# Node tables by one matmul and one-hots by one activation, laid out by DMA

## The chip, the cores and the metric

The kernel runs on one core of a Trainium2 chip. The metric is the device time of one execution in microseconds (us), and lower is better. The engines are TensorE (PE), VectorE (DVE), ScalarE (ACT), GpSimd (POOL) and SyncE (SP), which only issues DMAs and waits.

## The reference

The input x is 16 images of 96 channels, 64 x 64 points, float32. Two layers follow each other.

```python
# layer 0: graph convolution in windows of 8 x 8 points
y = affine(conv1x1(x, fc1_w, fc1_b), fc1_s, fc1_t)
nodes = window_partition(y)                    # 64 windows an image, each 64 nodes x 96
idx = knn_idx(nodes, 9)                        # nearest 9, by normalised dot products
x_j = nodes[idx]; x_i = nodes[:, None]
feat = concat([x_i, x_j - x_i])                # 192
h = gelu((feat @ ew.T + eb) * es + et)         # 192 outputs
h = max over the 9 neighbours
x1 = affine(conv1x1(h, fc2_w, fc2_b), fc2_s, fc2_t) + x
# layer 1: inverted bottleneck
h = relu(bn(conv1x1(x1, w1)))                  # 576 channels
h = relu(bn(depthwise_3x3(h, wd)))
out = x1 + bn(conv1x1(h, w2))
```

## The kernel before

The unit of work is a pair of windows, P, 128 nodes. There are 32 pairs an image and 512 in all. A loop over images holds one iteration of every engine per pair, in an order written out by hand, and only semaphores join the engines. Layer 1 works in strips of 16 rows (four an image), so a strip lasts eight pairs. Its jobs are put at fixed distances after the strip's first pair by tables such as `W1_AT`, `RELU2_AT`, `W2_AT`, `UPPER_AT`, `STORE_AT`. The place of a pair is its number mod 8. A place decides which of these jobs come in its iteration.

The edge convolution is split: every node has a row V (for itself as a neighbour) and a row U (as the centre), each 192 numbers. Neighbour k of node n gives V[idx] + U[n], and that sum is a matmul with a one-hot matrix: `VU` holds, per window, V on 64 partitions and U on the other 64. `MV` (128 partitions x 512 columns per window) holds the one-hots of the neighbours on 64 partitions and an eye matrix, written once in the set-up, on the other 64. In window 0 the one-hots stand on partitions 0 to 63, in window 1 on 64 to 127, and `VU` is arranged to match. Both are double-buffered by pair.

For one pair these steps follow each other over several iterations:

- `scores` (L588, three pairs ahead), then VectorE's eight largest, their indices and a feature; `feature_transpose` two pairs ahead.
- `expand` (L614), one pair ahead: eight small matmuls put, per neighbour, a number into the PSUM bank `pvu` (seen as `pone`) that is zero or below except where the index hits.
- `onehot` (L800) on ScalarE: two activations of 64 partitions, from that bank into the two halves of `MV`.
- `values` (L624), one pair ahead: four products, each of 64 nodes with V's or U's weights (192 columns), placed on the half of the same bank `pvu` where `VU` wants them. It waits for `onehot`, since that frees the bank.
- `vu_copy` (L812) on ScalarE: one activation of 128 x 384 from the bank into `VU`. The next `expand` waits for it.
- `gather` (L639), in three parts: parts 0 and 1 give 128 outputs of window 0 and window 1, part 2 the other 64 of both. ScalarE's GELU follows each part and VectorE takes the maxima.

An iteration on TensorE is: scores(P+3), gather part 0 of P, feature_transpose(P+2), the first of the shared jobs, expand(P+1), gather part 1, the other shared jobs, values(P+1), gather part 2. The shared jobs (`misc_jobs`: fc1, sums of squares, norms, the self terms, fc2, w1, w2) take three PSUM banks in turn.

GpSimd issues the accumulating DMAs: `acc<-tapped` (L429, 512 KB, four a strip), `res<-x` (L438) and `x<-in_x_dram` (L407), two of each a strip. SyncE issues everything else: the input loads, the norms' trip through DRAM and back, two copies a strip between halves of the 576 - 512 = 64 leftover channels (L374 to L381, `hpad` group 4) and the output stores (L389). ScalarE waits for the half-group copies by `kept_half` and for the stores by `store_done`.

## Time and profile before

| | |
|---|---|
| median of 3 runs | 4107.27 us (4103.47 to 4110.96) |
| profiled execution | 4102.94 us |
| its span, first to last instruction | 4101.1 us |
| mean granted TensorE clock | 0.987 |
| busy: TensorE, VectorE, ScalarE, GpSimd | 95%, 93%, 90%, 23% |
| DMA, mean | 66 GB/s |

A row of a group gives the line of the kernel, the engine, the tiles (out<-in), the shapes, the number of instructions, their busy time and mean duration, and the idle time of the engine just before them with what ended it. PE is the matmul itself and PEld its weight load. Each float32 product is two matmul instructions in the trace. The chain is the work that ended last, followed backwards. SPq is the DMA queue of SyncE. Durations of matmuls are modelled ends, so the distance between starts says more than a sum of them.

### The profile page before, as it was taken

To read this page: it belongs to the slowest core of one execution; us is meant where nothing else is said; L and a number is where in the kernel's file an instruction comes from. 1 tells how busy PE (TensorE), PEld (TensorE's weight loads), DVE (VectorE), ACT (ScalarE), POOL (GpSimd) and SP (SyncE) were. 2 spreads that over 40 slices of the span, in tenths; PEclk is the share of its full clock that TensorE was granted. 3 is DMA by queue.
4 is the path that set the end of the run, shared out by engine and by line. 5 is a ranking of instruction groups with operands and counts; after the bars stand their busy time and mean duration, and the time that the engine had idled before them with its cause. 6 is when DMAs were issued, how large, how long until landed. Compare 5 with 4: busy or idle time off the path is not lost.

```text
span 4101.1 us, 79112 instructions
## 1 busy us (share of the span) xinstructions
PE 3901.0 (95%) x22752; PEld 2049.0 (50%) x22752; DVE 3821.5 (93%) x5162; ACT 3694.2 (90%) x6805; POOL 931.2 (23%) x1060
## 2 busy tenths in 40 slices
PE   4999999999999999999999999999999999999984
PEld 2445555455554555555555455555555455555542
DVE  2599999999999999999999999999999999999996
ACT  3899999999998999989999899989999899999983
POOL 0122222122222122222122222122222122222113
PEclk9999999999999999999999999999999999999996
DMA  1133342333333333343333333333333333433333
GB/s 50 24 64 76 58 88 51 67 76 66 73 73 66 60 75 73 58 80 57 69 75 66 73 61 75 62 69 76 62 79 57 70 66 67 81 61 59 62 66 65
DMA packets 100114, 272.31 MB, mean 66 GB/s; under 512 B 14946, under 2 KB 23394, under 8 KB 93476
## 3 DMA queue, kind: packets, MB, share of 16 engines
q0 software_dynamic: 65536, 184.58, 26.4%
q1 hardware_dynamic: 34116, 82.27, 7.5%
q8 instruction: 204, 3.34, 0.3%
q14 instruction: 258, 2.11, 0.2%
HBM read 77.68 MB, written 25.69 MB: 25 GB/s over the span
## 4 chain that ended last, share of the span: by engine, by line
PE 68%; DVE 11%; issue 9%; ACT 9%; DMA 1%; SPq 0%; POOL 0%; DVEq 0%; ACTq 0%; POOLq 0%
PE pg L648 18%; PE pmisc L576 9%; PE pg L651 8%; PE pvu L635 8%; DVE acc L1032 7%; PE pmisc L562 7%; PE pmisc L519 3%; PE pmisc L512 2%; PE pvu L621 2%; ACT MV L807 2%; PE pmisc L578 2%; DVE hid L1010 2%; PE pmisc L542 2%; PE pmisc L547 2%; ACT tapped L844 1%
## 5 line engine op out<-in xcount | busy, mean ns | idle before, releaser
L1032 DVE SCALAR_TENSOR_TENSOR acc<-hpad,w,acc 128x1024 f32<-128x1024 f32 (+1 forms) x2304 | 2618.2, 1160 | 33.5 <-issue 16.3
L648 PE MATMUL pg<-MV,VU 128*128 128x512 f32 x2048 | 1149.2, 643 | 40.7 <-ACT VU L815 29.8
L824 ACT ACTIVATE g<-pg 128x512 f32<-128x512 f32 x1536 | 912.5, 594 | 127.9 <-PE pg L651 81.4
L1010 DVE TENSOR_REDUCE hid<-g 128x192 f32<-128x1536 f32 x512 | 892.6, 1743 | 0.0
L429 POOL DMA_DIRECT2D acc<-tapped x256 | 241.3, 943 | 2106.8 <-DVE acc L1032 1818.8
L807 ACT ACTIVATE MV<-pvu,cst 64x512 f32<-64x512 f32 x1024 | 696.0, 680 | 11.8 <-PE pvu L621 5.0
L576 PE MATMUL pmisc<-acc,w 128*96 128x256 f32 x2048 | 497.1, 386 | 49.0 <-ACT acc L854 34.1
L651 PE MATMUL pg<-MV,VU 128*64 128x512 f32 x2048 | 527.5, 592 | 0.0
L562 PE MATMUL pmisc<-x,w 96*128 96x512 f32 (+1 forms) x1024 | 518.3, 608 | 7.0 <-ACT hpad L766 7.0
L635 PE MATMUL pvu<-wVU,y 97*64 97x192 f32 x4096 | 446.7, 339 | 21.8 <-ACT MV L807 21.2
L576 PEld LDWEIGHTS pmisc<-acc,w 128*96 128x96 f32 x2048 | 331.5, 165 | 262.6 <-issue 154.9
L766 ACT ACTIVATE hpad<-pmisc,sh,sc 128x512 f32<-128x512 f32 (+1 forms) x560 | 421.6, 770 | 16.7 <-PE pmisc L562 9.0
L635 PEld LDWEIGHTS pvu<-wVU,y 97*64 97x64 f32 x4096 | 248.7, 136 | 300.8 <-issue 164.0
L854 ACT ACTIVATE acc<-acc,shd,scd 128x1024 f32<-128x1024 f32 (+1 forms) x320 | 360.6, 1147 | 29.6 <-DMA acc<-tapped 29.6
L648 PEld LDWEIGHTS pg<-MV,VU 128*128 128x128 f32 x2048 | 309.5, 191 | 87.3 <-issue 59.5
L837 ACT ACTIVATE acc<-hpad,w 128x1024 f32<-128x1024 f32 (+1 forms) x320 | 338.9, 1060 | 0.2
L600 PEld LDWEIGHTS pscore<-xn,xs 97*64 97x64 f32 x2048 | 145.9, 137 | 325.2 <-issue 315.6
L562 PEld LDWEIGHTS pmisc<-x,w 96*128 96x128 f32 x1024 | 185.7, 193 | 239.5 <-issue 214.2
L815 ACT ACTIVATE VU<-pvu 128x384 f32<-128x384 f32 x512 | 250.2, 489 | 51.2 <-PE pvu L635 40.5
L844 ACT ACTIVATE tapped<-hpad,w 128x1024 f32<-128x1024 f32 x256 | 292.2, 1141 | 0.0
L621 PEld LDWEIGHTS pvu<-featT,c 128*128 128x128 f16 x4096 | 183.0, 100 | 217.8 <-issue 214.7
L976 DVE MAX8 top<-pscore 128x8 f32<-128x64 f32 x512 | 115.9, 226 | 163.1 <-PE pscore L602 161.7
(101 smaller groups left out, 4447.6 us busy)
## 6 DMA issues: line engine op xcount, KB each, us to landing
acc<-tapped POOLq DMA_DIRECT2D x256, 512.0 KB, 4.9
xin<-in_x_dram SPq DMA_DIRECT2D x32, 768.0 KB, 5.8
invb<-rows_dram SPq DMA_DIRECT2D x32, 768.0 KB
x<-in_x_dram POOLq DMA_DIRECT2D x128, 192.0 KB, 4.4
res<-x POOLq DMA_DIRECT2D x128, 192.0 KB, 5.0
out_dram<-res SPq DMA_DIRECT2D x128, 192.0 KB, 3.2
hpad<-hpad SPq DMA_DIRECT2D x112, 33.0 KB, 1.8
g<-in_consts_dram SPq DMA_DIRECT2D x1, 640.0 KB
```

The costliest lines, as they stand in the source:

```text
L562: last = nc.tensor.matmul(ps[:, 0:(hi - lo) * W], w1T[:, gr * 128:(gr + 1) * 128], x1[:, lo:hi, :], start=True, stop=True)
L576: nc.tensor.matmul(ps[0:C, 0:4 * W], w2T[:, gr, :], acc[:, par, sums_of(gr, q * 4 * W, 4 * W)], start=(gr == 0), stop=False)
L635: last = nc.tensor.matmul(pvu[h:h + 64, O * w:O * (w + 1)], nodes, wVU[:, k, :], start=True, stop=True)
L648: last = nc.tensor.matmul(ps[:, :], VU[:, r, part, 0:ONE128], cols[part], start=True, stop=True)
L651: last = nc.tensor.matmul(ps[64 * w:64 * w + 64, :], VU[:, r, w, ONE128:O], cols[w], start=True, stop=True)
L766: nc.scalar.activation(hpad[:, gr, r0:r1, 1:W + 1], ps[:, 0:(r1 - r0) * W].rearrange("p (row col) -> p row col", col=W), ACT.Relu, bias=sh ...
L807: last = nc.scalar.activation(MV[h:h + 64, p % 2, w, :].rearrange("p (n k) -> p n k", k=KN), pone[h:h + 64, :, :].rearrange("p k n -> p n ...
L824: nc.scalar.activation(g[:, p % 2, part, :, :], pg[(3 * p + part) % 2][:, :].rearrange("p (n k) -> p n k", k=KN), ACT.Gelu).then_inc(gelu_ ...
L837: nc.scalar.activation(acc[:, t % 2, sums_of(gr, 0, rows * W)].rearrange("p (row col) -> p row col", col=W), hpad[:, gr, 0:rows, 0:W], ACT ...
L854: nc.scalar.activation(acc[:, par, sums_of(gr, 0, n)], acc[:, par, sums_of(gr, 0, n)], ACT.Relu, bias=shd[:, gr:gr + 1], scale=scd[:, gr:g ...
L1010: nc.vector.tensor_reduce(hid[:, c % 2, j, :, :], g[:, r], op=ALU.max, axis=AX.X).then_inc(hid_ready, 1)
L1032: nc.vector.scalar_tensor_tensor(out=dst, in0=src, scalar=wk, in1=dst, op0=ALU.mult, op1=ALU.add).then_inc(tap_done, 1)
```

## The change

- `values` is one product of 128 nodes with the weights of V and U side by side (384 columns). The result has the nodes on the partitions: window 0 on 0 to 63, window 1 on 64 to 127.
- `onehot` is one activation of 128 partitions, into a new tile `onehots`.
- `vu_copy` writes a new tile `nodesVU` instead of `VU`.
- SyncE puts both in place: `move_tables` with four DMAs (64 partitions x 192 numbers, 48 KB each) into `VU`, and `move_onehots` with two DMAs (64 partitions x 512 numbers, 128 KB each) into `MV`. The one-hots now stand on partitions 0 to 63 for both windows and the eye on 64 to 127. `onehots` and `nodesVU` are single, so `onehot` and `vu_copy` wait for the last moves.
- `values` and `vu_copy` run two pairs ahead instead of one. The bank `pvu` is still used in the order expand, values.
- The first gather of a pair waits for the two moves' semaphores instead of ScalarE's.
- In SyncE's order the moves come first in an iteration; the output stores and the upper half-group copy are one pair later, and the norms' trip is split over two pairs.
- `hpad` is stored as one run of rows, with 10 instead of 18 for the half group. The indexing follows (`rows_of`). VectorE's `last` gets a lower bound of 3.

```diff
@@ -42,7 +42,7 @@
 W1_AT = {-1: [(0, 0), (0, 1), (0, 2)], 0: [(1, 0)], 1: [(1, 1), (1, 2)], 2: [(2, 0), (2, 1), (2, 2)],
          3: [(3, 0), (3, 1), (3, 2)], 4: [(4, 0), (4, 2)]}
 KEEP_AT = {-2: (0, 1), 2: (2, 3)}
-UPPER_AT, LOWER_AT = {2: FULL}, {5: FULL}
+UPPER_AT, LOWER_AT = {3: FULL}, {5: FULL}
 TAP0_AT = {}
 TAP0_LATE = {0: [0], 1: [1], 3: [2], 4: [3], 5: [4]}
 RELU2_AT = {6: [0], 7: [1], 10: [2, 4], 11: [3]}
@@ -53,7 +53,7 @@
 SELF_AT = {2: 'self_half', 3: 'self_full', 4: 'self_half', 5: 'self_full'}
 ORDER = ('ssq', 'fc1', 'inv', 'self_full', 'self_half', 'fc2', 'w1', 'w2')
 ADD_AT = {o + 1: q for o, q in W2_AT.items() if q % 2 == 1}
-STORE_AT = {o + 2: q for o, q in W2_AT.items() if q % 2 == 1}
+STORE_AT = {o + 3: q for o, q in W2_AT.items() if q % 2 == 1}
 FIRST = [(g, k) for k in range(1, TAPS - 1) for g in (0, 1)]
 SECOND = [(2, 1), (3, 1), (2, 2), (3, 2), (4, 1), (2, 3), (3, 3), (4, 2), (2, 4), (4, 3), (3, 4), (2, 5), (4, 4), (3, 5),
           (2, 6), (4, 5), (3, 6), (2, 7), (4, 6), (3, 7), (4, 7), (4, 8)]
@@ -188,6 +188,11 @@
     return slice(g * STRIP * W + start, g * STRIP * W + start + n)
 
 
+def rows_of(g, first, end):
+
+    return slice((STRIP + 2) * g + first, (STRIP + 2) * g + end)
+
+
 def due(count):
 
...
@@ -263,6 +268,8 @@
         featT = sb("featT", [128, 2, NODES], f16)
         VU = sb("VU", [128, 2, 2, O])
         MV = sb("MV", [128, 2, 2, KN * NODES])
+        onehots = sb("onehots", [128, KN * NODES])
+        nodesVU = sb("nodesVU", [128, 2, O])
         g = sb("g", [128, 2, 3, NODES, KN])
         gself = sb("gself", [128, 2, PPC, 3, NODES])
         gflat = g[:, 0].rearrange("p c n k -> p (c n k)")
@@ -270,7 +277,7 @@
         r97 = g[0:C + 1, 1].rearrange("p c n k -> p (c n k)")[:, 0:3 * O]
         hid = sb("hid", [128, 2, PPC, 3, NODES])
         x1 = sb("x1", [C, H, W])
-        hpad = sb("hpad", [128, 5, STRIP + 2, PADW])
+        hpad = sb("hpad", [128, FULL * (STRIP + 2) + STRIP // 2 + 2, PADW])
         acc = sb("acc", [128, 2, (2 * FULL + 1) * STRIP * W // 2])
         tapped = sb("tapped", [128, FULL, STRIP * W])
         res = sb("res", [C, 2, CW])
@@ -298,6 +305,7 @@
             "score_ready", "top8_ready", "idx_ready", "a_ready", "feat_ready"))
         featT_ready, featT_evac, onehot_in, onehot_ready = (sem(n) for n in (
             "featT_ready", "featT_evac", "onehot_in", "onehot_ready"))
+        onehot_moved, vu_moved = sem("onehot_moved"), sem("vu_moved")
         vu_ready, vu_evac, gather_ready, gelu_done, chunk_ready = (sem(n) for n in (
             "vu_ready", "vu_evac", "gather_ready", "gelu_done", "chunk_ready"))
         kept, kept_half = sem("kept"), sem("kept_half")
@@ -337,13 +345,16 @@
             sp.dma_start(c16f[:, :], consts16).then_inc(param_load, 16)
             load_half(0, 1)
 
-            def broadcast_norms(b, p, bi, h):
-
-                n = 2 * bi + h
+            def store_norms(b, p, bi, h):
+
                 fb, fp = when(b, p, ROWS_AT - 8)
                 sp.wait_ge(misc_evac, job_at(fb, fp, "inv", 4 * h))
                 sp.sem_inc(sp_passed, 1)
                 sp.dma_start(rows_dram.rearrange("k (r n) -> (k r) n", n=128), norm_rows[:, :]).then_inc(rows_stored, 16)
+
+            def broadcast_norms(bi, h):
+
+                n = 2 * bi + h
                 sp.wait_ge(rows_stored, 16 * (n + 1))
                 sp.sem_inc(sp_passed, 1)
                 if due(count := 4 * n):
@@ -353,11 +364,37 @@
                 sp.dma_start(rows[0:C, :], rows_dram[0:1, :].to_broadcast([C, 4 * CW])).then_inc(rows_loaded, 16)
                 sp.dma_start(rows[C:C + 1, :], rows_dram[1:2, :]).then_inc(rows_loaded, 16)
 
+            def move_tables(P, p):
+
+                if due(count := 3 * P - 3):
+                    sp.wait_ge(gather_ready, count)
+                sp.sem_inc(sp_passed, 1)
+                if due(count := P + 1):
+                    sp.wait_ge(vu_evac, count)
+                sp.sem_inc(sp_passed, 1)
+                for k in range(2):
+                    for w in range(2):
+                        sp.dma_start(VU[64 * k:64 * k + 64, p % 2, w, :], nodesVU[64 * w:64 * w + 64, k, :]).then_inc(vu_moved, 16)
+
+            def move_onehots(P, p):
+
+                if due(count := P + 1):
+                    sp.wait_ge(onehot_ready, count)
+                sp.sem_inc(sp_passed, 1)
+                for w in range(2):
+                    sp.dma_start(MV[0:64, p % 2, w, :], onehots[64 * w:64 * w + 64, :]).then_inc(onehot_moved, 16)
+
             def image(b, p0, p1):
                 for p in range(p0, p1):
+                    P = PAIRS * b + p
                     h = 1 if p < 16 else 0
                     if p % 16 == ROWS_AT and valid(b if h else b + 1, B):
-                        broadcast_norms(b, p, b if h else b + 1, h)
+                        store_norms(b, p, b if h else b + 1, h)
+                    if p % 16 == ROWS_AT + 1 and valid(b if h else b + 1, B):
+                        broadcast_norms(b if h else b + 1, h)
+                    if valid(P + 1, NPAIRS):
+                        move_tables(P + 1, p + 1)
+                        move_onehots(P + 1, p + 1)
 
                     if p in (1, 8) and valid(b, B) and valid(b + 1, B):
                         h = p // 8
@@ -371,14 +408,14 @@
                             sp.wait_ge(tap_done, count)
                         sp.sem_inc(sp_passed, 1)
                         if t == 0:
-                            sp.dma_start(hpad[0:64, gr, 0, 1:W + 1], zrow[0:64, :]).then_inc(kept_half, 16)
+                            sp.dma_start(hpad[0:64, (STRIP + 2) * gr + 0, 1:W + 1], zrow[0:64, :]).then_inc(kept_half, 16)
                         else:
-                            sp.dma_start(hpad[0:64, gr, 0:2, :], hpad[64:128, gr, 8:10, :]).then_inc(kept_half, 16)
+                            sp.dma_start(hpad[0:64, rows_of(gr, 0, 2), :], hpad[64:128, rows_of(gr, 8, 10), :]).then_inc(kept_half, 16)
                     for o, t, s, gr in due_in(LOWER_AT, b, p):
                         fb, fp = when(b, p, o - w1_slot(gr, 0))
                         sp.wait_ge(misc_evac, job_at(fb, fp, "w1", (gr, 0)))
                         sp.sem_inc(sp_passed, 1)
-                        sp.dma_start(hpad[64:128, gr, 0:2, :], hpad[0:64, gr, 8:10, :]).then_inc(kept_half, 16)
+                        sp.dma_start(hpad[64:128, rows_of(gr, 0, 2), :], hpad[0:64, rows_of(gr, 8, 10), :]).then_inc(kept_half, 16)
 
                     for o, t, s, q in due_in(STORE_AT, b, p):
                         sp.wait_ge(out_sum[q // 2], 16 * (s + 1))
...
@@ -615,7 +652,7 @@
                 if due(count := P + 1):
                     pe.wait_ge(featT_evac, count)
 
-                if due(count := P):
+                if due(count := P + 1):
                     pe.wait_ge(vu_evac, count)
                 for k in range(KN):
                     last = nc.tensor.matmul(pone[:, k, :], LK[:, k, :], featT[:, p % 2, :], start=True, stop=True)
@@ -625,15 +662,10 @@
 
                 c, o = pair(p)
 
-                if due(count := P + 1):
+                if due(count := P):
                     pe.wait_ge(onehot_ready, count)
-                for w in range(2):
-                    nodes = y[:, c, o + NODES * w:o + NODES * (w + 1)]
-                    for k in range(2):
-
-                        h = 64 * (w ^ k)
-                        last = nc.tensor.matmul(pvu[h:h + 64, O * w:O * (w + 1)], nodes, wVU[:, k, :], start=True,
-                                                stop=True)
+                last = nc.tensor.matmul(pvu[:, 0:2 * O], y[:, c, o:o + 128], wVU[:, 0:2, :].rearrange("p k o -> p (k o)"),
+                                        start=True, stop=True)
                 last.then_inc(vu_ready, 1)
 
             def gather(P, p, part):
@@ -664,10 +696,10 @@
                     if valid(P + 3, NPAIRS):
                         scores(b, P + 3, p + 3)
                     if valid(P, NPAIRS):
-                        if due(count := P + 1):
-                            pe.wait_ge(onehot_ready, count)
-                        if due(count := P + 1):
-                            pe.wait_ge(vu_evac, count)
+                        if due(count := 32 * (P + 1)):
+                            pe.wait_ge(onehot_moved, count)
+                        if due(count := 64 * (P + 1)):
+                            pe.wait_ge(vu_moved, count)
                         gather(P, p, 0)
                     if valid(P + 2, NPAIRS):
                         feature_transpose(P + 2, p + 2)
@@ -681,8 +713,8 @@
                         shared_job(b, p, k, jobs[k])
                     for k in part_of(jobs, 2) + part_of(jobs, 3):
                         shared_job(b, p, k, jobs[k])
-                    if valid(P + 1, NPAIRS):
-                        values(P + 1, p + 1)
+                    if valid(P + 2, NPAIRS):
+                        values(P + 2, p + 2)
                     if valid(P, NPAIRS):
                         gather(P, p, 2)
 
...
@@ -800,19 +832,16 @@
             def onehot(P, p):
                 act.wait_ge(onehot_in, P + 1)
 
-                if due(count := 3 * P - 3):
-                    act.wait_ge(gather_ready, count)
-                for w in range(2):
-                    h = 64 * w
-                    last = nc.scalar.activation(MV[h:h + 64, p % 2, w, :].rearrange("p (n k) -> p n k", k=KN),
-                                                pone[h:h + 64, :, :].rearrange("p k n -> p n k"), ACT.Relu,
-                                                bias=nbias[h:h + 64, :], scale=1.0)
-                last.then_inc(onehot_ready, 1)
+                if due(count := 32 * P):
+                    act.wait_ge(onehot_moved, count)
+                nc.scalar.activation(onehots[:, :].rearrange("p (n k) -> p n k", k=KN), pone.rearrange("p k n -> p n k"),
+                                     ACT.Relu, bias=nbias, scale=1.0).then_inc(onehot_ready, 1)
 
             def vu_copy(P, p):
                 act.wait_ge(vu_ready, P + 1)
-                r = p % 2
-                nc.scalar.activation(VU[:, r, :, :], pvu[:, 0:2 * O].rearrange("p (win o) -> p win o", win=2),
+                if due(count := 64 * P):
+                    act.wait_ge(vu_moved, count)
+                nc.scalar.activation(nodesVU[:, :, :], pvu[:, 0:2 * O].rearrange("p (k o) -> p k o", k=2),
                                      ACT.Copy).then_inc(vu_evac, 1)
 
             def gelu(P, p, part):
...
@@ -886,8 +915,8 @@
                         shared_evac(b, p, k, jobs[k])
                     for k in part_of(jobs, 2) + part_of(jobs, 3):
                         shared_evac(b, p, k, jobs[k])
-                    if valid(P + 1, NPAIRS):
-                        vu_copy(P + 1, p + 1)
+                    if valid(P + 2, NPAIRS):
+                        vu_copy(P + 2, p + 2)
                     if valid(P + 3, NPAIRS):
                         feature_square(P + 3, p + 3)
                     if valid(P, NPAIRS):
...
@@ -939,7 +968,7 @@
 
             for r in range(2):
                 for w in range(2):
-                    u = 64 * (1 - w)
+                    u = 64
                     step(nc.vector.tensor_copy(MV[u:u + 64, r, w, :].rearrange("p (n k) -> p n k", k=KN),
                                                eye[u:u + 64, :].unsqueeze(2).to_broadcast([64, NODES, KN])))
 
...
@@ -1039,7 +1068,7 @@
                     new = valid(P + 3, NPAIRS)
                     h = 1 if p < 16 else 0
                     bi = b if h else b + 1
-                    last = min(len(taps) - 1, 4) if p % PPC == 0 else 4
+                    last = max(3, min(len(taps) - 1, 4)) if p % PPC == 0 else 4
 
                     for a in taps[0:2]:
                         tap(*a)
```

## Rows read from the trace of the kernel before

**Rows 1.** The page: busy time and share of each engine, and the chain that ended last.
```profile
PE 3901.0 (95%) x22752; PEld 2049.0 (50%) x22752; DVE 3821.5 (93%) x5162; ACT 3694.2 (90%) x6805; POOL 931.2 (23%) x1060
...
PE 68%; DVE 11%; issue 9%; ACT 9%; DMA 1%; SPq 0%; POOL 0%; DVEq 0%; ACTq 0%; POOLq 0%
```

**Rows 2.** Windows: stretch, length, busy us of PE, PEld, DVE, ACT, POOL, clock, DMA share, GB/s.
```profile
2000.00:3000.00 1000.00, 981.60 (x5765) 517.08 (x5765) 963.66 (x1300) 933.60 (x1722) 234.15 (x269) 0.99 0.36 69
```

**Rows 3.** Groups of instructions by line and shape: busy us, mean ns, idle before.
```profile
L807 ACT ACTIVATE MV<-pvu,cst 64x512 f32<-64x512 f32 x1024 | 696.0, 680 | 11.8 <-PE pvu L621 5.0
...
L635 PE MATMUL pvu<-wVU,y 97*64 97x192 f32 x4096 | 446.7, 339 | 21.8 <-ACT MV L807 21.2
```

**Rows 4.** Chain in order of time, 2000 to 2040 us: start, us, what.
```profile
2004.42 0.80 PE pvu L635 x8
...
2009.43 0.86 PE pmisc L562 x2
```

**Rows 5.** Waits of the whole span: us in total, times, longest.
```profile
PE pg L648 <- ACT VU L815: 29.8, 57, 0.8
...
PE pvu L635 <- ACT MV L807: 21.2, 57, 1.6
```

**Rows 6.** Timeline, a pair of place 1: start, us, engine, line.
```profile
2024.69 0.89 POOL L429 DMA_DIRECT2D acc<-tapped  x1 [18.25 <-DVE acc L1032]
...
2025.05 1.37 ACT L807 ACTIVATE MV<-pvu,cst 64x512 f32<-64x512 f32 x2
...
2025.31 1.11 POOL L438 DMA_DIRECT2D res<-x  x1
...
2028.47 1.12 PE L648 MATMUL pg<-MV,VU 128*128 128x512 f32 x2
```

**Rows 7.** Timeline, pairs of place 0 and place 5: one-hots and next first gather.
```profile
2018.07 1.37 ACT L807 ACTIVATE MV<-pvu,cst 64x512 f32<-64x512 f32 x2
...
2021.36 1.12 PE L648 MATMUL pg<-MV,VU 128*128 128x512 f32 x2
...
2055.07 1.36 ACT L807 ACTIVATE MV<-pvu,cst 64x512 f32<-64x512 f32 x2
...
2059.14 1.12 PE L648 MATMUL pg<-MV,VU 128*128 128x512 f32 x2
```

**Rows 8.** Timeline, two pairs of place 6, the later one with fc1 first.
```profile
2061.53 1.38 ACT L807 ACTIVATE MV<-pvu,cst 64x512 f32<-64x512 f32 x2 [0.16 <-PE pvu L621]
...
2067.11 1.13 PE L648 MATMUL pg<-MV,VU 128*128 128x512 f32 x2
...
2123.60 0.88 POOL L429 DMA_DIRECT2D acc<-tapped  x1
...
2123.91 1.36 ACT L807 ACTIVATE MV<-pvu,cst 64x512 f32<-64x512 f32 x2
...
2127.52 1.12 PE L648 MATMUL pg<-MV,VU 128*128 128x512 f32 x2
```

**Rows 9.** DMA issues in windows at 2009, 2031, 2049 and 2029 us: us to landing.
```profile
out_dram<-res SPq DMA_DIRECT2D x1, 192.0 KB, 2.1
...
out_dram<-res SPq DMA_DIRECT2D x1, 192.0 KB, 4.8
...
hpad<-hpad SPq DMA_DIRECT2D x1, 33.0 KB, 1.8
...
hpad<-hpad SPq DMA_DIRECT2D x1, 33.0 KB, 3.8
```

**Rows 10.** Timeline: the contended copy of rows 9 and the DMA issued ahead of it.
```profile
2028.94 1.67 POOL L429 DMA_DIRECT2D acc<-tapped  x1
...
2029.72 0.47 SPq L376 DMA_DIRECT2D hpad<-hpad  x1
```

**Rows 11.** The page: DMA queues, packets, MB, share of 16 engines' span.
```profile
q0 software_dynamic: 65536, 184.58, 26.4%
q1 hardware_dynamic: 34116, 82.27, 7.5%
```

24 lines of the change are left out of this document (12 added, 12 removed).

## Prediction

> **What bounds the kernel now.** I read the busy row and the chain first: TensorE is busy 95% and holds 68% of the chain that ended last; VectorE is busy 93%, ScalarE 90% [rows 1]. Then the windows, to keep the middle apart from the ends. In 2000 to 3000 us TensorE is idle 18.4 us of 1000, VectorE 36, ScalarE 66, and the granted clock is 0.99 of full speed, the 2.4 GHz level [rows 2]. So in the steady part TensorE's stream sets the pace, one pair of windows about every 7.7 us, with VectorE close behind: if TensorE alone gets faster, VectorE is full after 3.6%. ScalarE and the queues matter through what TensorE waits for at a gather.
>
> **The table product.** Eight matmul instructions of 192 columns per pair (four products, two instructions each) become two of 384 columns. The eight hold the chain for 0.80 us; two of 512 columns hold it for 0.86 us [rows 4]. Two of 384 take 384/512 of that, 0.65 us. Bounds: 0.65, and 0.86 (no better than 512 columns). I take 0.66, so 0.14 us gained for each of the 512 pairs (4096 instructions / 8 [rows 3]): 72 us.
>
> **The one-hots.** Two ScalarE instructions of 64 partitions, 680 ns each [rows 3], become one of 128 partitions. Bounds: 0.68 us, if only columns count, and 1.36, if partitions did; I take 0.68, the row with the same columns: ScalarE loses 348 us of work. At 1.36 nothing is lost or won on ScalarE, and the times left below shrink by 0.68 us. TensorE waited for them 21.2 us before the product, and 29.8 us for the table copy before the first gather [rows 5]. The product moves one pair ahead, so both waits end: 51 us. ScalarE's other saved time lies beside TensorE and is worth nothing by itself; TensorE's steady idle of 18.4 in 1000 us, about 64 over 3500, caps what all removed waits can give [rows 2].
>
> **The new link.** So far the gather of pair P+1 could start when the second one-hot instruction had ended. Now the one-hots must pass SyncE, two DMAs of 128 KB, and their semaphore. For the wait that this adds, I put two times side by side: what the kernel *leaves* between the end of the first one-hot instruction (where the single one will end) and the first gather of the next pair, and what the move *needs*.
>
> *Left*, by the pair's place in the eight pairs of a strip. Place 0: the one-hots start at 2018.07, +0.69 is 2018.76, the gather starts at 2021.36: 2.6 us [rows 7]. Place 1: 2025.74 to 2028.47, 2.7; without its waits and with the shorter product TensorE comes there about 0.5 us sooner, so 2.2 [rows 6]. Place 5: 2055.76 to 2059.14, 3.4 [rows 7]. Place 6 alternates: where fc1's two ScalarE instructions stand before the one-hots, 2124.60 to 2127.52, 2.9; in the other half 2062.22 to 2067.11, 4.9 [rows 8]. From each, 0.14 goes for the shorter product.
>
> *Needed*, calm. A copy of 33 KB between 64 partitions lands 1.8 us after its issue, a store of 192 KB after 2.1 [rows 9]; the first of two issues takes 0.47 us [rows 10]. 0.47 + 2.1 = 2.6 us. That fits, but for place 1 (0.4 short) and half of place 0 (0.1 short).
>
> *Needed*, beside the accumulating DMAs of GpSimd. This is the step that decides. The same 33 KB copy lands after 3.8 us when issued 0.8 us behind such a DMA, the same 192 KB store after 4.8 [rows 9]. So 0.47 + 3.8 = 4.3 to 0.47 + 4.8 = 5.3 us. The skill gives a reason, and it speaks against this change. The Trainium skill, DMA: Bandwidth & Descriptors, section "Issuing engines are not separate DMA queues", says that DMAs of all issuing engines end up on the same 16 DMA engines and interleave; by that rule, the trace agrees: 2.1 against 4.8. A second rule, in the Trainium skill, SBUF — State Buffer, section "Door 1: The DMA port swizzle", says that partitions 0 to 63 reach only 8 of the 16 ports, some 218 GB/s; an estimate from that page for 256 KB is 1.2 us where the profile's rates give 1.0, which would raise the sum by 0.2 us x 64 to 128 = 13 to 26 us, and no run here shows it.
>
> Where do they meet? Place 1: acc and res DMAs issued 1.0 and 0.4 us before the one-hots end [rows 6], a third behind them: 4.3 - 2.2 = 2.1 us of stall (0.4 to 3.1). I take the lower end of the range, since VectorE, less pressed, can issue its DMA up to a microsecond sooner. Place 6: the acc DMA is issued 1.0 us before the end [rows 8]: 4.3 - 2.8 = 1.5 us, in half of the periods, 0.75 (0 to 1.2). Places 2 and 5 lie at the edge of such a DMA: 0.2 each (0 to 1.0 each). Place 0: 0.05. What is behind the stalled gather on TensorE is the transpose, the first shared products and the next expansion; ScalarE's GELU and, a pair later, VectorE's maxima wait for them, and nothing overtakes, so a stall moves the whole period. The waits added on ScalarE (one-hots and table copy for the buffers' last moves) cost nothing: the gathers have waited for the same moves before. Sum 2.1 + 0.75 + 0.4 + 0.05 = 3.3 us per eight pairs, 64 periods: 211 us. Bounds: 0.45 x 64 = 29 and 6.3 x 64 = 400.
>
> **Costed at nothing.** The four table moves (192 KB a pair) are issued about when a pair starts, with a whole pair before their reader; if that cover went, each would be a stall like the above. They add traffic: q1 now moves 82.27 MB in 7.5% of the engines' time [rows 11], and (256 + 192) KB x 512 is 235 MB more, 21 points of share on 34; that is why I don't use the low bounds. SyncE's queue is now paced by the pairs: its six issues at 0.47 us are 2.8 us of 7.7. Behind its wait for the one-hots stand the output stores, the input loads, the norms and the two half-group copies. The stores and the upper copy were moved one pair later; the norms' broadcast leaves one pair later and is needed a pair after that. The lower copy now leaves after the one-hots of place 5 and is awaited by ScalarE at that pair's end, with some 3 us left against 1.8 to 3.8 needed: nothing to 1 us per period, inside the bound of place 5. The memsets, the smaller hpad and the eye rows are set-up; the new `last` changes nothing where four or more taps are due. At the start the first gather waits once for a move, 3 us.
>
> **Sum.** The profiled execution took 4102.9 us (span 4101.1), 4.4 below the median of 4107.3. 4102.9 - 72 - 51 + 211 = 4191; with the 4 us to the median, 4195 us.
>
> **Rivals.**
> *The moves share evenly.* 256 KB at q1's rate (82.27 MB in 7.5% of 16 x 4101 us, 16.7 KB per us and engine [rows 11]) is 1.0 us; if the other queue only halved that rate, the need would be 3.6: 1.4 + 0.4 + 0.1 + 0.05 = 1.95 us per period, 125 us: 4107 - 123 + 125 = 4109. For it: two queues and a modest mean load. Against: 33 KB, a quarter of one move, was already held back 2.0 us [rows 9].
> *The moves are hidden (the other side).* Place: the first gather of a pair. If VectorE's DMAs come so early that only place 1 and place 0 are short, the stall is 0.45 us per period, 29 us: 4107 - 123 + 29 = 4013, faster by 2.3%. It decides when the stalls per period fall below 123/64 = 1.9 us. For it: the DMA engines are busy 34% in mean [rows 11], so most moves should find them free. Against: 33 KB at 3.8, in the places where the rows show the DMAs.
> *Worse than forecast.* The table moves stretch GpSimd's DMAs, so places 2 and 5 stall by 1 us too, or SyncE's stores hold the next move: 2.1 + 1.2 + 2.0 + 0.05 = 5.3 us, 342 us: 4107 - 123 + 342 = 4326. The stalls are of 1 to 3 us, between long busy stretches; if the clock fell to the 1.2 GHz level behind them, it would be worse still.
> *The change doesn't do what it says.* The product at 0.86 us would lose 0.06 x 512 = 31 us rather than gain 72; it shifts every case by 100 us. I give it nothing of its own.
>
> **Chances.** A measurement of this kernel tells 0.2% (8 us) from no change. Forecast, the contended moves stall the gathers, 0.46 (own range 4120 to 4280). Even sharing, 4109 give or take 50: 0.26, of which 0.14 faster, 0.08 same, 0.04 slower. Hidden: 0.20. Worse: 0.08. So faster 0.34, same 0.08, slower 0.58. The range: 4010 leaves out half of "hidden", 4290 leaves out "worse": 4010 to 4290.
>
> **What would show it.** The product's two instructions hold the chain for 0.65 us; ScalarE's busy time near 3350 us; no wait of the product for the one-hots. Against these a new row, TensorE's first gather waiting for the DMA of the one-hots, some 200 us in 100 to 200 times, in places 1 and 6, and none in places 3, 4 and 7. DMA share from 34 to about 55%. I am wrong if the moves land in under 3 us beside an accumulating DMA, if SyncE arrives late at its wait for the one-hots, or if TensorE's gain is taken by VectorE waiting for nothing.

## The result: slower by 16.5%, and the profile after

The changed kernel takes 4784.9 us (median of 4 runs, 4776.5 to 4789.0), against 4105.4 us (4101.3 to 4111.0) for the kernel before in runs beside it: ratio 1.165, 95% interval 1.163 to 1.167. I forecast 4195 us in a range of 4010 to 4290. The direction is right, the size is not: +680 us where the sum of the prediction gave +88.

The page of the changed kernel, against [rows 1, 11]:

```profile
span 4774.7 us, 78907 instructions
PE 4216.4 (88%) x19680; PEld 2078.5 (44%) x19680; DVE 3836.2 (80%) x5162; ACT 3381.1 (71%) x6293; POOL 941.2 (20%) x1060
PEclk9989899899899898898998899998998999998997
q1 hardware_dynamic: 279876, 317.35, 27.1%
q0 software_dynamic: 65536, 184.58, 22.6%
PE 64%; DMA 18%; ACT 8%; issue 5%; SPq 3%; DVE 2%; ACTq 0%; POOL 0%; POOLq 0%
```

Two things to see. DMA went from 1% to 18% of the chain. And TensorE is busy for 315 us *more* than before with 3,072 fewer instructions: work does not explain that, a lower clock can, and the clock row shows eights through the whole span. Its mean is 0.912 of full speed, before 0.987. The groups, waits and DMA issues, against [rows 3, 5, 9]:

```profile
L680 PE MATMUL pg<-MV,VU 128*128 128x512 f32 x2048 | 1270.3, 705 | 438.6 <-DMA MV<-onehots 426.1
L837 ACT ACTIVATE onehots<-pvu,cst 128x512 f32<-128x512 f32 x512 | 351.5, 687 | 22.7 <-PE pvu L658 21.7
L667 PE MATMUL pvu<-wVU,y 97*128 97x384 f32 x1024 | 440.5, 512 | 2.6 <-ACT onehots L837 2.5
```
```profile
DVE top L1005 <- PE pscore L639: 818.5, 299, 12.9
PE pg L680 <- DMA MV<-onehots: 426.1, 198, 6.8
```
```profile
MV<-onehots SPq DMA_DIRECT2D x1024, 128.0 KB, 2.4
acc<-tapped POOLq DMA_DIRECT2D x256, 512.0 KB, 5.2
VU<-nodesVU SPq DMA_DIRECT2D x2048, 48.0 KB, 2.2
```

The median move lands in 2.4 us, near the 2.1 us forecast for a calm one. The stall comes from the few that don't, above all the one that is issued in place 1 and awaited in place 2. Windows there (columns as in [rows 2]), with TensorE's timeline and, behind it, SyncE's and GpSimd's issues:

```profile
1996.00:1999.00 3.00, 3.00 (x18) 1.50 (x16) 3.00 (x6) 3.00 (x7) 1.73 (x2) 1.00 0.65 133
1999.00:2006.30 7.30, 2.37 (x14) 0.90 (x12) 6.90 (x11) 4.43 (x7) 3.00 (x4) 0.96 1.05 182
2006.30:2013.00 6.70, 6.65 (x25) 3.61 (x25) 3.37 (x3) 2.09 (x5) 0.00 (x0) 0.50 0.97 214
2013.00:2020.00 7.00, 7.00 (x20) 2.46 (x16) 0.00 (x0) 2.66 (x7) 0.00 (x0) 0.55 0.13 31
2020.00:2027.00 7.00, 6.79 (x35) 2.96 (x31) 6.67 (x10) 6.69 (x13) 1.41 (x1) 1.00 0.31 70
```
```profile
2001.17 0.20 PE L639 MATMUL pscore<-c 128*64 128x64 f16 x2
2006.35 2.07 PE L680 MATMUL pg<-MV,VU 128*128 128x512 f32 x2 [4.98 <-DMA MV<-onehots]
...
2010.40 2.06 PE L680 MATMUL pg<-MV,VU 128*128 128x512 f32 x2
...
2020.00 1.12 PE L680 MATMUL pg<-MV,VU 128*128 128x512 f32 x2
```
```profile
1999.09 1.72 SPq L385 DMA_DIRECT2D MV<-onehots  x2
2001.16 1.96 SPq L426 DMA_DIRECT2D out_dram<-res  x1
```
```profile
1996.36 0.89 POOL L466 DMA_DIRECT2D acc<-tapped  x1 [16.22 <-DVE acc L1061]
1996.97 1.11 POOL L475 DMA_DIRECT2D res<-x  x1
...
1999.15 0.79 POOL L444 DMA_DIRECT2D x<-in_x_dram  x1 [1.06 <-ACT x L775]
...
2001.26 0.88 POOL L466 DMA_DIRECT2D acc<-tapped  x1
```

From the first issue of the one-hots (1999.09) to the gather (2006.35) it is 7.3 us, where 4.3 to 5.3 were forecast; the DMA engines are full in that stretch (1.05). It is no single case: over some 50 strips this distance is 7.4 us in the mean. Behind the stall of 4.98 us the same instructions take 2.07 us instead of 1.12: after 5 idle us the granted clock is 0.50, the 1.2 GHz level, and only at 2020 back at 1.00.

Where the time is, by a tabulation of my own: from the timeline I took each pair's first gather, start to start, for some 50 strips between 400 and 3900 us. Idle ahead of the first gather, and pair length, by place (mean us):

```
place                 0      1      2      3      4      5      6      7     sum
idle, before        -.02   -.02    .27    .04    .41    .00   -.02   -.02
idle, after          .00    .25   5.06    .00    .21    .00    .55    .77    6.8
length, before      7.58   7.22   7.47   7.59   8.13   7.54   7.54   8.44   61.5
length, after       7.62  11.80  12.56   7.52   8.11   8.13   8.37   8.10   72.2
length, no moves    7.34   6.76   7.40   7.16   8.12   7.53   7.52   8.14   60.0
```

The move issued in place 1 is awaited at place 2's first gather, which closes place 1's length. After minus before is 10.7 us a strip, x 64 = 685 us. The row "no moves" is the first experiment. It splits the changed kernel's strip: 60.0 + 6.8 of idle + 5.2 by which place 2 is longer (12.56 against 7.40) = 72.0, measured 72.2. In 46 of 49 strips that pair's first gather runs at half clock, and its second in all 49.

### The profile page after: what moved, and what is told of

Same layout as the page of the kernel before. It is cut to its first block, busy times and chain, and to the rows that moved or that the text cites. A ratio compares the mean times of both kernels' runs of the same rounds, so it can differ in the third digit from the quotient of the medians.

```text
span 4774.7 us, 78907 instructions
## 1 busy us (share of the span) xinstructions
PE 4216.4 (88%) x19680; PEld 2078.5 (44%) x19680; DVE 3836.2 (80%) x5162; ACT 3381.1 (71%) x6293; POOL 941.2 (20%) x1060
## 4 chain that ended last, share of the span: by engine, by line
PE 64%; DMA 18%; ACT 8%; issue 5%; SPq 3%; DVE 2%; ACTq 0%; POOL 0%; POOLq 0%
PE pg L680 18%; DMA MV<-onehots 17%; PE pmisc L599 9%; PE pg L683 7%; PE pmisc L613 7%; PE pvu L667 5%; PE pmisc L556 3%; ACT onehots L837 3%; PE pvu L658 2%; PE pmisc L584 2%; SPq L385 2%; PE pmisc L549 2%; PE pmisc L615 2%; DVE acc L1061 2%; PE pmisc L579 2%
## 5 line engine op out<-in xcount | busy, mean ns | idle before, releaser
L680 PE MATMUL pg<-MV,VU 128*128 128x512 f32 x2048 | 1270.3, 705 | 438.6 <-DMA MV<-onehots 426.1
L599 PE MATMUL pmisc<-x,w 96*128 96x512 f32 (+1 forms) x1024 | 587.3, 681 | 7.7 <-ACT hpad L798 7.7
L683 PE MATMUL pg<-MV,VU 128*64 128x512 f32 x2048 | 567.3, 633 | 0.0
L680 PEld LDWEIGHTS pg<-MV,VU 128*128 128x128 f32 x2048 | 336.5, 206 | 491.8 <-issue 334.9
L667 PE MATMUL pvu<-wVU,y 97*128 97x384 f32 x1024 | 440.5, 512 | 2.6 <-ACT onehots L837 2.5
L837 ACT ACTIVATE onehots<-pvu,cst 128x512 f32<-128x512 f32 x512 | 351.5, 687 | 22.7 <-PE pvu L658 21.7
L844 ACT ACTIVATE nodesVU<-pvu 128x384 f32<-128x384 f32 x512 | 251.6, 491 | 121.4 <-PE pvu L667 72.8
L599 PEld LDWEIGHTS pmisc<-x,w 96*128 96x128 f32 x1024 | 210.2, 218 | 289.4 <-issue 249.6
L508 POOL COPY xs<-xn 96x512 f32<-96x512 f32 x128 | 160.0, 1250 | 793.5 <-DVE xn L1033 793.5
L658 PEld LDWEIGHTS pvu<-featT,c 128*128 128x128 f16 x4096 | 197.0, 104 | 223.3 <-issue 218.9
```

Of the source, the lines that this page charges most:

```text
L599: last = nc.tensor.matmul(ps[:, 0:(hi - lo) * W], w1T[:, gr * 128:(gr + 1) * 128], x1[:, lo:hi, :], start=True, stop=True)
L667: last = nc.tensor.matmul(pvu[:, 0:2 * O], y[:, c, o:o + 128], wVU[:, 0:2, :].rearrange("p k o -> p (k o)"), start=True, stop=True)
L680: last = nc.tensor.matmul(ps[:, :], VU[:, r, part, 0:ONE128], cols[part], start=True, stop=True)
L683: last = nc.tensor.matmul(ps[64 * w:64 * w + 64, :], VU[:, r, w, ONE128:O], cols[w], start=True, stop=True)
L837: nc.scalar.activation(onehots[:, :].rearrange("p (n k) -> p n k", k=KN), pone.rearrange("p k n -> p n k"), ACT.Relu, bias=nbias, scale=1. ...
```

## The experiments

All are edits of the changed kernel, and every ratio is to the kernel before, on the same chip. The first theory: moves land late beside GpSimd's DMAs, and the clock falls behind the stall. Counts of strips are my own, from timelines between 400 and 3900 us.

**1. No moves.** SyncE's moves and the waits for them go.
```diff
-                        move_tables(P + 1, p + 1)
-                        move_onehots(P + 1, p + 1)
...
-                        if due(count := 32 * (P + 1)):
-                            pe.wait_ge(onehot_moved, count)
+                        if due(count := P + 1):
+                            pe.wait_ge(onehot_ready, count)
```


> The changed kernel without the six moves (the gathers read tables and one-hots that are set to zero once in the set-up, so their content is left out) and with the gathers waiting for ScalarE again. It leaves the compute side of the change alone. Theory (all of the loss comes from the moves): 72 us from the shorter product and up to 51 us from the removed waits, 3985 to 4035 us. Rival (the product of 384 columns or the new order costs time itself): 4100 us or more.


Measured 4010.4 us, 0.977 (0.976 to 0.979): the theory's range. All 775 us above that come with the moves and the waits for them. But the gain of 94 us isn't the product's: places 4, 5 and 6, where TensorE waits for nothing, are as long as before (table). It lies in places 0, 1, 2, 3 and 7, 1.5 us a strip, where waits ended. The product's two instructions do take 0.81 us in the timeline, and eight took 0.87:
```profile
2017.23 0.59 PE L612 MATMUL pmisc<-acc,w 128*96 128x256 f32 x2
2017.66 0.81 PE L664 MATMUL pvu<-wVU,y 97*128 97x384 f32 x2
2018.40 1.08 PE L680 MATMUL pg<-MV,VU 128*64 128x512 f32 x4
2019.31 0.29 PE L634 MATMUL pscore<-xn,xs 97*64 97x64 f32 x4
```
From the start of w2's last part to that of the scores it is 2.08 us here and 2.08 before (2019.03 to 2021.11).

**2, 3. One half of the moves each.** In 2 ScalarE writes MV itself in two 64-partition instructions; in 3 four products lay the tables in place.
```diff
-                        move_onehots(P + 1, p + 1)
```
```diff
-                last = nc.tensor.matmul(pvu[:, 0:2 * O], y[:, c, o:o + 128], wVU[:, 0:2, :].rearrange("p k o -> p (k o)"),
...
+                        last = nc.tensor.matmul(pvu[64 * k:64 * k + 64, O * w:O * (w + 1)], nodes, wVU[:, k, :],
```


> The changed kernel with the one-hots undone: two ScalarE instructions write them straight into their halves as before; the tables still come from the one product, one pair sooner, by four DMAs. Theory (the one-hot moves alone are late, since their reader comes 3 to 4 us behind them, while the tables have a whole pair): the stalls of 5 us and the halved clock behind them are gone, the product's gain stays, 4020 to 4070 us. Rival (it is the DMA traffic as such, to which the tables give two thirds of the rows): 4200 us or more.

> The other half undone: four products and a ScalarE copy straight into the tables, one pair ahead, as before; the one-hots by one instruction and two DMAs. Theory (one-hot moves are the cause): the stall in place 1 and the halved clock stay, 4600 to 4850 us. Rival (the table moves delay the one-hot moves, or the traffic does it): under 4300 us.


With the one-hots direct (2) it is 4324.8 us, 1.053 (1.051 to 1.055); with the tables direct (3) 4739.7 us, 1.156 (1.154 to 1.158). So the one-hot moves carry nearly all, as expected of 3. But on 2 the theory missed (4070 us at most) and the time lies in the rival's range: with the table moves alone the kernel is still 220 us above the kernel before.
```profile
ACT nodesVU L847 <- DMA VU<-nodesVU: 192.2, 77, 5.7
PE pg L679 <- DMA VU<-nodesVU: 156.4, 49, 5.8
```
By pair of the image, the stall of the first gather stands at pairs 3, 11 and 27 (1.9, 3.9, 4.3 us) and is 0.2 at 19. SyncE's 768 KB transfers go into its queue around the first three, and none around pair 19.

**4. Does the clock cost by itself?** Twelve dummy instructions on TensorE fill the wait in place 2.
```diff
+                        if p % 8 == 2:
+                            for _ in range(6):
+                                nc.tensor.matmul(pfeat[:, 64:512], eye128[:, :], w128[:, 0:448], start=True, stop=True)
```


> The changed kernel with six further products of 448 columns (about 4.5 us at the full clock) on TensorE ahead of the one gather in eight that stalls by 5 us; their result is read by nobody. Theory (half of the loss is TensorE's clock, which falls during the stall and runs the next 12 us at half speed): the filler lies in the stall, the clock stays up, and 64 x 4 to 5 us come back, 4470 to 4550 us, although 290 us of work are added. Rival (the clock record is a side effect, and the pair after the stall is long because its transfers are late too): 4785 us or more, up to 5070 us.


Measured 4565.9 us, 1.112 (1.109 to 1.114): with 4.78 us of work *added* per strip the kernel got 219 us faster. The pair behind is 8.76 us instead of 12.56, at half clock in 1 strip of 51.
```profile
2000.00:3000.00 1000.00, 958.00 (x4673) 475.97 (x4672) 871.23 (x1167) 770.21 (x1439) 210.05 (x242) 0.99 0.54 115
```
```profile
2050.45 4.78 PE L701 MATMUL pfeat<-w,eye 128*128 128x448 f32 x12
2055.29 1.12 PE L680 MATMUL pg<-MV,VU 128*128 128x512 f32 x2
```
All of the DMA traffic is still there, so it isn't the traffic that takes the clock down. I had expected 4550 at most; places 3 and 7 now wait 1.1 and 0.9 us, and in 11 pairs of these strips, in places 2, 3 and 7, the second gather is still at half clock.

**5, 6. Whose traffic is in the way?** The accumulating DMA of 512 KB cut to 64 columns; then the DMAs for x and res.
```diff
-                nc.gpsimd.dma_start(acc[:, t % 2, sums_of(gr, 0, STRIP * W)], tapped[:, gr, :],
+                nc.gpsimd.dma_start(acc[:, t % 2, sums_of(gr, 0, W)], tapped[:, gr, 0:W],
```
```diff
-                nc.gpsimd.dma_start(res[:, q // 2, :], x1v[:, c * CW:(c + 1) * CW],
+                nc.gpsimd.dma_start(res[:, q // 2, 0:W], x1v[:, c * CW:c * CW + W],
```


> The changed kernel with GpSimd's accumulating acc DMAs cut to one row of 64 of their 1024 columns (the rest of the last tap's sum is left out); their number, order and waits stay. Theory (the one-hot moves are held back beside these transfers on the same engines): the gap of 5.1 us ahead of place 2's first gather falls under 1 us, the clock stays up, 4030 to 4130 us. Rival (the moves are slow by their own issues on SyncE and by going to 64 partitions): the gap stays above 4 us, above 4650 us.

> The changed kernel with GpSimd's other DMAs, the additions of x and of x1, cut to 64 of 512 columns (the rest of both additions is left out). Of the four DMAs around the one-hot move of place 1 two are nearly empty. Theory (the move lasts as long as what is queued beside it): the gap before place 2's first gather falls from 5.1 to about 2.5 us, in part of the periods without the fall of the clock, 4300 to 4550 us. Rival (as for the acc DMAs): above 4650 us.


5 took 4496.6 us, 1.095 (1.093 to 1.097), and 6 took 4461.8, 1.085 (1.083 to 1.088). The first misses its theory (4130 at most), the second lies in its range. Neither DMA is the single cause: the stall in place 2 is 3.0 and 2.1 us. In 5 the stalls of places 6 and 7 nearly go too, from 0.55 and 0.77 us to 0.2 and 0.1.

These two runs also say what the clock costs behind shorter stalls. Place 2's first gather is at half clock in only 20 of 51 and 11 of 52 strips, but its second one in 51 of 51 and 34 of 52. The pair is 12.0 and 10.6 us long instead of 7.4 (0.3 of the 10.6 is the next pair's wait): 4.6 us more behind a stall of 3.0, and 2.9 more behind one of 2.1.

**7. Ports.** The moves write both halves of the partitions.
```diff
-                    sp.dma_start(MV[0:64, p % 2, w, :], onehots[64 * w:64 * w + 64, :]).then_inc(onehot_moved, 16)
+                    sp.dma_start(MV[64 * w:64 * w + 64, p % 2, w, :], onehots[64 * w:64 * w + 64, :]).then_inc(onehot_moved, 16)
```


> The changed kernel with window 1's one-hots moved to partitions 64 to 127 instead of 0 to 63 (and its eye, U and V changed over), so that the two one-hot DMAs write both halves of the partitions. Same bytes, same number of DMAs. Theory: the transfers beside it decide, so under 3% of the time moves, 4650 to 4790 us. Rival (64 partitions reach half of the ports, and both moves share that half): the landing of the second move gets 0.5 us or more sooner everywhere, under 4600 us.


4761.7 us, 1.160 (1.158 to 1.162), in the theory's range: 23 us or 0.5% under the changed kernel.

**8. One-hots a pair sooner too.**
```diff
-                    if valid(P + 1, NPAIRS):
-                        expand(P + 1, p + 1)
...
+                    if valid(P + 2, NPAIRS):
+                        expand(P + 2, p + 2)
```


> The changed kernel with the one-hots one pair sooner too: expansion and one-hots of pair P+2 in iteration P, behind the second gather, and their move at the start of the next iteration, ahead of the tables' move. The move then has some 7 us before its reader instead of 3 to 4. Theory (what the moves lack is time): the gap of place 2 falls to 0 to 3 us and the halved clock goes for the most part, 4080 to 4350 us. Rival (the moves' traffic in the crowded stretch costs the same wherever it stands): 4600 us or more.


4867.2 us, 1.184 (1.181 to 1.187). The theory missed and the time lies in the rival's range, but the run doesn't show the rival's reason. `onehots` and `nodesVU` are single buffers, and ScalarE now waits for the moves out of them (352 us for the tables, 348 for the one-hots; in the changed kernel 46 and none); the stall in place 2 is down to 2.6 us.

**9, 10, 11. Small other traffic.** 10 cuts SyncE's 768 KB transfers to 64 columns; 9 does that and the cuts of 5 and 6; 11 is experiment 2 with the cut of 10.
```diff
-                        load_half(b + 1, h)
+                        sp.dma_start(xin[:, h, 0:64], xv[b + 1, :, h * 4 * CW:h * 4 * CW + 64]).then_inc(xin_load[h], 16)
```


> The changed kernel with all other large transfers cut: GpSimd's acc DMAs and its two additions to 64 columns, and SyncE's 768 KB input loads and norm broadcasts (after the first) to 64 columns; what they would have brought is left out. The moves are whole. Theory (the moves are late only beside other transfers; by themselves they need 2.6 us and have 2.2 to 4.9): 4020 to 4080 us against 4010 us without moves, no fall of the clock. Rival (the six issues and the hop over SyncE are too slow in themselves): above 4150 us.

> The changed kernel with only SyncE's own 768 KB transfers (input loads, norm broadcasts) cut to 64 columns; the rest of them is left out. Theory (they stand in the same queue around pairs 1, 2, 10 and 26 of 32, and those pairs are longer than pair 18, which has GpSimd's DMAs alone): the gap of 5.1 us before place 2 goes only to about 4.4, the pairs of place 2 lose about 1 us, 4600 to 4720 us. Rival (GpSimd's DMAs do harm only together with them): under 4450 us.

> One-hots direct, tables by DMA (4325 us) and SyncE's 768 KB transfers cut to 64 columns as before. Theory (the table moves are late only where a 768 KB transfer stands ahead of them in SyncE's queue: the pairs 2, 3, 10, 11, 26 and 27 of 32 are long, 18 and 19 are not): all periods become like those, 4080 to 4140 us. Rival (GpSimd's DMAs alone make the tables late): above 4230 us.


10: 4772.3 us, 1.163 (1.160 to 1.165): a miss (4720 at most was expected), as good as no effect. 11: 4096.5 us, 0.997 (0.995 to 0.998): the 220 us of experiment 2 come from these 768 KB transfers. The two fit together: in the changed kernel the one-hots' stall comes at place 2, one pair earlier, and place 3 no longer waits (0.00 in the table). That the one covers the other is my reading, not a run of its own. 9: 4214.1 us, 1.025 (1.023 to 1.027), above my theory (4080 at most) and in the rival's range: even with all other traffic small, the moves cost 204 us over none. Idle ahead of first gathers sums to 2.1 us a strip (1.4 of it at place 2), 136 us. The rest, some 70 us, is the clock again, behind far shorter waits (place 2's pair is 8.7 us long instead of 7.4):
```profile
1265.46 1.12 PE L681 MATMUL pg<-MV,VU 128*128 128x512 f32 x2 [1.68 <-DMA MV<-onehots]
1267.97 2.06 PE L681 MATMUL pg<-MV,VU 128*128 128x512 f32 x2
```
The gather behind the wait is still at full speed, the next one at half. Of 59 waits of 0.9 us or more (mean 1.3) 24 went so, with 10.2 us for the pair behind; the other 35 had 7.5.

**12, 14, 15. Bytes or rows.** 12: moves of 64 and 24 columns. 14: moves of 16 of 64 partitions. 15: as 9, with GpSimd's DMAs on 16 partitions.
```diff
-                    sp.dma_start(MV[0:64, p % 2, w, :], onehots[64 * w:64 * w + 64, :]).then_inc(onehot_moved, 16)
+                    sp.dma_start(MV[0:16, p % 2, w, :], onehots[64 * w:64 * w + 16, :]).then_inc(onehot_moved, 16)
```


> The changed kernel with its own moves cut to an eighth of the bytes, 64 of 512 one-hot columns and 24 of 192 table columns (the rest of both stays zero), in the same six DMAs with the same number of rows. Everything else is whole. Theory (a row of a move waits for rows of the other queue, so rows count and not bytes; the acc DMAs cut to a sixteenth of their bytes still left a gap of 3 us): the gap before place 2 stays above 3 us, above 4450 us. Rival (the 229 MB of the moves are the cost): under 4250 us.

> The changed kernel with its moves cut to 16 of 64 partitions each, all columns (the rest of tables and one-hots stays zero): a quarter of the rows and of the bytes, one row for each engine and DMA. Beside e_few_bytes (all rows, an eighth of the bytes, 4570 us, gap 3.5 us). Theory (every row of a move waits for one of the other queue): the gap falls under 2 us, under 4400 us. Rival (a move waits a fixed time behind what the other queue has in flight, whatever its size): the gap stays above 3 us, above 4500 us.

> The kernel with all other large transfers cut (4214 us) and GpSimd's DMAs cut further, from all partitions to 16 (nearly all of the additions is left out), so that hardly a row stands beside the moves. Theory (what is left of the gap in place 2, 1.4 us, is for the greater part the move's own time against the time left): 4150 to 4210 us. Rival (the small rows held the moves back): under 4110 us.


In the order 12, 14, 15: 4570.4 us, 1.114 (1.111 to 1.118); 4593.7, 1.121 (1.119 to 1.122); 4149.1, 1.011 (1.009 to 1.012). The theory of 12 held. That of 14, that every row of a move waits for one of the other queue, missed (4400 at most); its rival held, a wait that hardly depends on the move's size. With an eighth of the bytes or a quarter of the rows the stall of place 2 is 3.5 us both times, of 5.06. So a third of it goes with the moves' size; in experiment 9, with whole moves and the others' transfers cut, all but 1.4 goes. The two savings overlap.

Experiment 15 lies 0.9 us under its range. It shows what the new link costs by itself: with hardly a row beside them, the moves still cost 139 us over none (4149.1 against 4010.4), and place 2 still stalls by 1.0 us. From SyncE's first issue of the one-hots to the gather that waits for them it is 3.5 us here (3.4 in the median of the strips):
```profile
2055.64 1.10 SPq L386 DMA_DIRECT2D MV<-onehots  x2
```
```profile
2059.13 1.12 PE L681 MATMUL pg<-MV,VU 128*128 128x512 f32 x2 [1.04 <-DMA MV<-onehots]
```

**13. The made-up stall.** No moves; in place 2 TensorE waits for four 4 KB DMAs, one after the other.
```diff
+                    if p % 8 == 1 and valid(b, B):
+                        sp.wait_ge(onehot_ready, P + 2)
+                        sp.sem_inc(sp_passed, 1)
+                        for k in range(4):
+                            sp.dma_start(scratch[:, :], cst[0:16, 81:145]).then_inc(vu_moved, 16)
```


> The kernel without moves (4010 us; the gathers' tables and one-hots are zeros, left out as there) with one made-up wait: in place 1 SyncE issues, after the one-hots, four DMAs of 4 KB one after the other, each awaited, and the first gather of place 2 waits for the last. TensorE stalls by some 5 us in one pair of eight, with no traffic to speak of. Theory (a stall of this length is paid twice, once as idle time and once by the halved clock behind it): 8 to 10 us a period, 4520 to 4660 us. Rival (only the idle time counts, the rest of the loss was traffic): 64 x 5 = 320 us, 4300 to 4370 us.


4942.6 us, 1.204 (1.202 to 1.206). The wait came out at 9.6 us where I had meant 5, so the time lies above both ranges that I had given.
```profile
1995.00:2005.00 10.00, 0.16 (x8) 0.02 (x2) 8.56 (x11) 2.67 (x3) 0.00 (x0) 0.69 0.55 92
2005.00:2012.00 7.00, 6.93 (x25) 4.02 (x26) 0.00 (x0) 1.96 (x5) 0.00 (x0) 0.50 0.20 59
```
```profile
2005.07 2.07 PE L686 MATMUL pg<-MV,VU 128*128 128x512 f32 x2 [9.91 <-DMA scratch<-cst]
...
2016.10 1.12 PE L686 MATMUL pg<-MV,VU 128*128 128x512 f32 x2
```
A strip is 14.6 us longer than in experiment 1 ((4942.6 - 4010.4) / 64): 9.6 of idle and 5.3 in the pair behind (12.71 against 7.40) make 14.9 in the middle of the run; in the first three strips the wait is 5 us. The first gather behind it is at half clock in all 47 strips. The clock adds the same behind a stall of 9.6 us as behind one of 5 (5.2 us). A wait without the kernel's moves brings the price too, so the moves' traffic isn't needed for it.

**16. A version from the findings.** Experiment 2, with the table moves first in SyncE's turn, and the 768 KB transfers away from the crowded pairs.
```diff
-                    if p in (1, 8) and valid(b, B) and valid(b + 1, B):
+                    if p in (3, 11) and valid(b, B) and valid(b + 1, B):
```


> A complete kernel: one-hots direct, tables by the one product and DMA, and SyncE's 768 KB transfers whole but elsewhere: the input loads in pairs 3 and 11 behind the tables' moves, the norms' trip in pairs 8 and 24, one pair sooner. Theory (the tables were late only behind these transfers in the crowded stretch): as with the transfers cut (4096 us), 4085 to 4125 us, so at least level with the kernel before. Rival (they do the same harm wherever they stand, or are now late for fc1 and the norms): above 4180 us.


4096.6 us, 0.998 (0.997 to 0.999): 0.2% under the kernel before, at the edge of what can be told from no change. It takes back 228 us of experiment 2 by the order and place of the transfers alone; none of them is smaller.

## Why the prediction was wrong in size

**Right.** The mechanism and the place: the new link through SyncE, a gather that waits for the one-hots' DMA in place 1's move above all. ScalarE: 687 ns for 128 partitions, 3381 us in all (forecast 3350); the same columns on 64 partitions took 680 ns, so here only columns counted. The product's wait for the one-hots shrank from 21.2 to 2.5 us.

**The step that failed first: "*Needed*, beside the accumulating DMAs", 4.3 to 5.3 us.** It was 7.3 us, and place 1's stall 5.06 us instead of 2.1; those of places 5, 6 and 0 came to 0.55, 0.77 and 0.25 us instead of 0.2, 0.75 and 0.05 (in the table they stand at the place behind). All stalls: 6.8 us a strip instead of 3.3, 438 us instead of 211. I priced the move with [rows 9], one copy or store beside one to three transfers of GpSimd. In the changed kernel place 1's move meets two accumulating DMAs, x and res (experiments 5 and 6 each give back part), and the DMA engines are full for 14 us; the two halves of the move land 5.3 and 6.6 us after their issue (median of the strips), where I had taken 3.8 and bounded it by 4.8. The calm need was too small as well: 3.4 us in experiment 15, not 2.6. So even the rival "hidden", at 29 us, wasn't open: with hardly any other traffic the moves cost 139. I also took the lower end of my own bounds, for a reason (VectorE issues sooner) that no run bore out. The Trainium skill, DMA: Bandwidth & Descriptors, section "Issuing engines are not separate DMA queues", says that all engines' DMAs share the 16 DMA engines. The move at 7.3 us, and at 3.5 with the others cut, agrees; the page gives no size.

**The step that was left out of the sum: the clock.** It stood in one line of the rival "worse" ("if the clock fell to the 1.2 GHz level behind them"), with no price. It is 5.2 us a strip, 333 us, half of the result. Experiments 4 and 13 show it from two sides: filling the idle time removes most of it, a wait of another origin brings it. The stalls of 2.1 us that I forecast would not have been free of it either: in experiment 6, with stalls of 2.1 us in place 2, the pair behind is 2.9 us longer. That is 186 us over 64 strips, and in experiment 9 four in ten waits of about 1.3 us were followed by 2.8 us.

**The product, -72 us, gained nothing.** I read the chain's 0.80 us for the eight and scaled 0.86 by columns. In the timeline the stretch around the product is 2.08 us before and in experiment 1 (medians of 238 such places: 2.09 and 2.08). Eight instructions of 192 columns on half of the TensorE columns were no slower than two of 384; the truth, 0.81 us in the timeline, is nearer to my rival of 0.86 than to 0.66. Why was not tried. The Trainium skill, TensorEngine Tiling (Array Packing), section "Key Properties", says that different tiles can run matmuls in parallel, which would explain it; no run here shows it.

**Removed waits, 51 us: they are 94 to 96.** I counted the matmuls' idle column of [rows 5] alone. The weight load that goes ahead of the product waited too, and the view of waits of the kernel before had it in a row that I hadn't used:
```profile
PEld pvu L635 <- ACT MV L807: 113.2, 133, 2.4
```
Experiment 1's 94 us come from waits only. So the two terms are -72 - 51 = -123 forecast and -94 measured: nearly right by luck, two errors that cancel.

**"Costed at nothing", the table moves.** Nearly right in the changed kernel (experiments 3 and 10: 45 us and 13 us), wrong by itself (experiment 2: 220 us). Their cover of a whole pair goes at pairs 3, 11 and 27, behind a 768 KB transfer in SyncE's queue, and stays at pair 19. That transfer was in the text only as something "behind its wait".

**The sum again, with what was measured:** 4105 - 94 + 438 + 333 = 4782; measured 4785. The two large terms are read from the changed kernel's own trace, so this closes the account and is no second test of it; the tests are experiments 1, 4 and 13.

**Ports.** The estimate from the Trainium skill, SBUF — State Buffer, section "Door 1: The DMA port swizzle", was 13 to 26 us; experiment 7 gave back 23. The size agrees and is small. That the ports are the reason isn't shown: experiment 7 changes the tables' destinations too.

**Still open:** what exactly holds a small move behind GpSimd's transfers. With neither its bytes nor its rows does it go below 3.5 us of stall, and cutting the rows of GpSimd's DMAs (experiment 15 against 9) gives back 65 us. Whether it is the number of their pieces in flight or something in SyncE's issue, where the pair of issues took 1.72 us in the crowded stretch and 1.10 in experiment 15, wasn't separated.

## What to carry to other kernels

A DMA put between two engines' steps is priced where the queues are fullest, with the kernel's own new traffic added there, and not at its median landing. Where TensorE sets the pace, add a price for the clock behind each wait: here some 5 us behind one of 5 or 9.6 us, 4.6 behind one of 3.0, 2.9 behind one of 2.1, and 2.8 behind four in ten of 1.3. Before counting a gain from fewer and wider matmuls, look for the start-to-start distance of their neighbours in the timeline, and read the weight loads' waits beside the matmuls'.

## What the runs showed that I had not expected

- One idle wait of 5 us on TensorE, and one of 9.6 us, are followed by the 1.2 GHz level and a pair longer by 5.2 and 5.3 us (12.6 and 12.7 against 7.4).
- Shorter stalls cost almost as much behind them: a pair longer by 4.6 us behind a mean stall of 3.0 us, by 2.9 behind one of 2.1.
- Waits of only 1.3 us were followed by it in 24 of 59 cases, from the second gather behind the wait on (10.2 us for the pair against 7.5).
- Adding 4.8 us of matmuls per strip made the kernel 219 us faster.
- A move of 16 KB that lands in 1.8 us in the median lands after 4.0 to 5.0 us in the crowded stretch (medians of the first and second), and 7.7 at most; one of 128 KB in 2.4, 5.3 to 6.6 and 8.5 us.
- Two 97x128 by 384 product instructions fill as much of TensorE's time as eight 97x64 by 192 (2.08 us for the stretch around them).
